# Feed-forward pass: gathers moved between POOL's power and its additions, a broadcast tensor operand on VectorE, and a later turn of h in the gated layers

## The reference

```
edge_index = jnp.stack([src, dst])
x = _layernorm(x + _L0_gnn_ref(x, edge_index, edge_attr_32, ...), axis=-1)
x = _layernorm(x + _L1_gnn_ref(x, edge_index, ...), axis=-1)
x = _layernorm(x + _L2_gnn_ref(x, ..., edge_index), axis=-1)
x = _layernorm(x + _L3_gnn_ref(x, edge_index, L3_gnn_weight), axis=-1)

# _L0_gnn_ref, after attention; `out` is the attended sum of each node
x = layer_norm(x + out, ln1_g, ln1_b)
h = x @ f1W + f1b
h = jax.nn.gelu(layer_norm(h, lnf_g, lnf_b), approximate=False)
h = h @ f2W + f2b
x = layer_norm(x + h, ln2_g, ln2_b)

# _L2_gnn_ref
h = x @ lin_w.T + lin_b
for i in range(3):
    m = h @ weight[i]
    agg = jax.ops.segment_sum(m[src], dst, num_segments=n_nodes)
    h = gru_cell(agg, h, w_ih, w_hh, b_ih, b_hh)   # (1 - z) * n + z * h
```

## Time and profile before

| | us |
|---|---|
| median of 3 runs | 6031.04 |
| the 3 runs | 6031.04, 6014.32, 6034.06 |
| profiled execution, its own time | 6028.9 |
| span of its instructions | 6027.0 |
| mean granted TensorE clock (share of 2.4 GHz) | 0.867 |

### The profile page before, as it was taken

How to read it: one execution, slowest core, us unless ns; L and a number is a source line. 1 busy time by engine, 2 the same in 40 slices (tenths; PEclk the granted TensorE clock), 3 DMA queues, 4 the chain that set the end, 5 groups by cost and what they waited for, 6 DMA issues and landing times. The chain is left out here.

```text
span 6027.0 us, 75672 instructions
## 1 busy us (share of the span) xinstructions
PE 4279.1 (71%) x16190; PEld 2524.1 (42%) x16190; DVE 4070.7 (68%) x13522; ACT 2924.8 (49%) x6388; POOL 3629.7 (60%) x3234
## 2 busy tenths in 40 slices
PE   6577759999997556546665679967996669836643
PEld 3244434444443333334443445534443334336643
DVE  6576659999997444457775676557665889836633
ACT  0466637777775010146665345534443446536643
POOL 4676558888885888735555660056104757855355
PEclk8788869999998777778887899988998899977877
DMA  6233323333332444456665675457545667757621
GB/s 214 66 85 80 73 70 99 99 99 99 99 99 78 62 62 63 54 141 196 193 190 162 185 211 146 131 160 214 164 141 147 176 159 211 197 162 227 183 78 54
DMA packets 767598, 802.43 MB, mean 133 GB/s; under 512 B 139632, under 2 KB 527800, under 8 KB 767018
## 3 DMA queue, kind: packets, MB, share of 16 engines
q1 hardware_dynamic: 405354, 393.44, 23.5%
q0 software_dynamic: 117504, 209.42, 15.0%
q10 hardware_dynamic: 244288, 194.72, 9.7%
HBM read 445.32 MB, written 351.92 MB: 132 GB/s over the span
## 5 line engine op out<-in xcount | busy, mean ns | idle before, releaser
L462 PE MATMUL gate_bank<-gate_ht,gate_whh 128*128 128x512 f32 x1764 | 874.6, 618 | 32.5 <-DVE gate_n L532 22.2
L925 POOL DMA_INDIRECT xh<-mean_xh,mean_pos_all x392 | 378.0, 964 | 349.0 <-DVE mean_xh L1027 158.9
L462 PEld LDWEIGHTS gate_bank<-gate_ht,gate_whh 128*128 128x128 f32 x1764 | 341.3, 202 | 413.0 <-issue 381.6
L2053 PE MATMUL back_ps_sums<-back_same,back_rows 128*128 128x512 f32 x400 | 289.5, 890 | 285.7 <-DMA back_rows<-x_a,back_idx 285.7
L151 POOL DMA_INDIRECT ffn_rows<-att_sums,ffn_idx x392 | 409.0, 1043 | 114.8 <-issue 106.3
L289 POOL DMA_INDIRECT gate_rows<-h_a,by_pos x200 | 195.8, 979 | 433.3 <-POOLq L117 327.3
L1494 PE MATMUL ffn_ps_f<-ffn_hg,ffn_f 128*128 128x512 f32 x784 | 407.1, 616 | 46.4 <-ACT ffn_hg L1671 46.4
L458 PE MATMUL gate_bank<-by_rank,gate_win 128*128 128x512 f32 x882 | 435.1, 593 | 0.0
L1487 PE MATMUL ffn_ps_u<-ffn_xs_t,ffn_up_w 128*128 128x512 f32 x784 | 387.2, 596 | 1.1 <-issue 1.1
L583 ACT ACTIVATE gate_z<-gate_bank,gate_b_rz 128x512 f32<-128x512 f32 x294 | 201.5, 686 | 351.0 <-PE gate_bank L462 221.0
L2034 POOL DMA_INDIRECT back<-back_out,back_dest x200 | 324.3, 1621 | 68.0 <-issue 60.1
(11 more groups left out here) (270 smaller groups left out, 11984.1 us busy)
## 6 DMA issues: line engine op xcount, KB each, us to landing
mean_x<-x_a SPq DMA_DIRECT2D x196, 256.0 KB
back<-blank ACTq DMA_DIRECT2D x99, 264.0 KB, 4.6
mean_rows<-back SPq DMA_DIRECT2D x98, 264.0 KB
hp<-mean_xh SPq DMA_DIRECT2D x98, 264.0 KB
gate_x<-xh SPq DMA_DIRECT2D x98, 264.0 KB
gate_hot<-hot_rows SPq DMA_DIRECT2D x100, 256.0 KB
ffn_x<-in_x_in SPq DMA_DIRECT2D x98, 256.0 KB
ffn_xr<-in_x_in SPq DMA_DIRECT2D x98, 256.0 KB
```

The source lines that it names most:

```text
L462: last = nc.tensor.matmul(bank_[:, :], whh[:, c * D:(c + 1) * D], ht[:, t.slot4, :], start=not inputs, stop=True)
L925: nc.gpsimd.indirect_dma_start(out=g["xh"][:, :], out_offset=bass.IndirectOffsetOnAxis(ap=pos_all[:, t.n, j:j + 1], axis=0), in_=xh[:, t.n ...
L2053: last = nc.tensor.matmul(ps_sums[t.slot][:, :], rows[:, t.slot4, j, :], same[:, t.slot, j, :], start=j == 0, stop=j == J - 1)
```

## The change

In `ffn_pass`, POOL's gathers of tile s go to the front of its step; since the steps follow each other, they now stand between the power of the step before and the two additions. DVE makes `xh` with `scalar_tensor_tensor`, whose second operand is the column of `inv` broadcast over 128 columns, where it was `tensor_scalar` with that column as a scalar.

In `gated_layer`, PE turns `hn` of item_at(3) instead of item_at(2), and all that follows comes a step later: the copies and stores, in gate2 the addition, statistics, power, shift, application, reload and scatter. `hn` gets four slots instead of two. The steps at the end grow by one.

```
@@ gated_layer
-        d, hn = (f.sb(s, [P, 2, SUPER]) for s in ("d", "hn"))
+        d, hn = f.sb("d", [P, 2, SUPER]), f.sb("hn", [P, 4, SUPER])
...
-        stored, ht_stored = f.sems("stored"), f.sems("ht_stored")
+        stored, ht_stored = f.sems("stored"), f.sems("ht_stored", 4)
...
-                if final and (t := item_at(5)) and t.has:
+                if final and (t := item_at(6)) and t.has:
                     wait(sp, stored[t.m % 2], 16 * (t.m // 2 + 1))
                     wait_alone(sp, back_scattered[t.m % 4], 64 * (t.m // 4))
                     sp.dma_start(back_x[:, t.m % 4, :, :], part_tile(x_out, HT + t.m, 0, D)
...
-                if final and (t := item_at(5)):
+                if final and (t := item_at(6)):
                     ln.rstd(nc, pool, t, y_done)
                 if e := edges_at(0):
                     sums.gather(pool, e)
-                if final and (t := item_at(6)) and t.has:
+                if final and (t := item_at(7)) and t.has:
...
-                if t := item_at(2):
+                if t := item_at(3):
                     wait(pe, h_done, t.n + 1)
                     wait(pe, out_done, t.n)
                     for j in range(J):
                         last = nc.tensor.transpose(ps_out[:, j * D:(j + 1) * D],
-                                                   hn[:, t.slot, j * P:(j + 1) * P], g["ident"][:, :])
+                                                   hn[:, t.slot4, j * P:(j + 1) * P], g["ident"][:, :])
...
-                    wait(dve, h_turned, t.n - 1)
+                    wait(dve, h_turned, t.n - 3)
                     if not final:
-                        wait(dve, ht_stored[t.slot], 16 * t.u)
+                        wait(dve, ht_stored[t.slot4], 16 * t.u4)
...
-                if final and (t := item_at(5)):
+                if final and (t := item_at(6)):
                     ln.shifts(nc, dve, t, y_done)
-                if final and (t := item_at(2)):
+                if final and (t := item_at(3)):
                     wait(dve, h_turned, t.n + 1)
...
-                if not final and (t := item_at(2)):
+                if not final and (t := item_at(3)):
                     wait(act, h_done, t.n + 1)
-                    act.dma_start(ht_out[t.tile], hn[:, t.slot, :]).then_inc(ht_stored[t.slot], 16)
+                    act.dma_start(ht_out[t.tile], hn[:, t.slot4, :]).then_inc(ht_stored[t.slot4], 16)
@@ ffn_pass
             def step(tile_at):
+                if t := tile_at(0):
+                    gather_step(nc, pool, t, idx, rows, g["att_sums"], idx_loaded, a_done, gathered)
                 if t := tile_at(2):
                     wait(pool, gathered[t.slot4], 64 * (t.u4 + 1))
...
-                if t := tile_at(0):
-                    gather_step(nc, pool, t, idx, rows, g["att_sums"], idx_loaded, a_done, gathered)
...
-                        last = nc.vector.tensor_scalar(xh[:, t.slot4, j, :], a[:, t.slot4, j, :],
-                                                       mv[:, root_slot(t, LN1), LN1, j, 0:1], inverse(t, LN1)[:, j:j + 1],
-                                                       ALU.subtract, ALU.mult)
+                        last = nc.vector.scalar_tensor_tensor(
+                            xh[:, t.slot4, j, :], a[:, t.slot4, j, :], mv[:, root_slot(t, LN1), LN1, j, 0:1],
+                            inverse(t, LN1)[:, j:j + 1].broadcast_to([P, D]), ALU.subtract, ALU.mult)
```

More of the change, by code:

```diff
@@ L420, in step @@
                                  ).then_inc(back_loaded[t.m % 4], 16)
-            over_items(5 if final else 0, step)
+            over_items(6 if final else 0, step)
             if initial:
@@ L444, in step @@
                             in_=back_x[:, t.m % 4, j, :], in_offset=None).then_inc(back_scattered[t.m % 4], 16)
-            over_items(6, step)
+            over_items(7 if final else 0, step)
             if final:
@@ L498, in step @@
                     sums.sum(pe, e)
-            over_items(2, step)
+            over_items(3, step)
         @block.vector
@@ L521, in step @@
                     wait(dve, d2_done, t.n + 1)
-                    wait(dve, h_turned, t.n - 1)
+                    wait(dve, h_turned, t.n - 3)
                     if not final:
-                        wait(dve, ht_stored[t.slot], 16 * t.u)
-                    nc.vector.tensor_tensor(hn[:, t.slot, :], d[:, t.slot, :], n3[:, t.slot, :],
+                        wait(dve, ht_stored[t.slot4], 16 * t.u4)
+                    nc.vector.tensor_tensor(hn[:, t.slot4, :], d[:, t.slot, :], n3[:, t.slot, :],
                                             ALU.add).then_inc(h_done, 1)
@@ L556, in step @@
                     nc.vector.tensor_copy(g["node_at"][:, HT:NT, :], g["tails"][:, HT:NT, :, 0]).then_inc(ids_made, 1)
-            over_items(5 if final else 2, step)
+            over_items(6 if final else 2, step)
         @block.scalar
@@ L572, in step @@
                                          ).then_inc(id_done, 1)
-                if final and (t := item_at(6)):
+                if final and (t := item_at(7)):
                     wait(act, stored[t.slot], 16 * t.u)
@@ L602, in step @@
                     nc.scalar.activation(ht[:, t.slot4, :], ps_in[:, :], ACT.Copy).then_inc(ht_made, 1)
-                if final and (t := item_at(6)):
+                if final and (t := item_at(7)):
                     wait(act, y_done, t.n + 1)
                     act.dma_start(part_tile(x_out, t.tile, 0, D), y[:, t.slot, :, :]).then_inc(stored[t.slot], 16)
-            over_items(6 if final else 2, step)
+            over_items(7 if final else 3, step)
             for b in range(2):
                 act.wait_ge(stored[b], 16 * (NT // 2))
-                if not final:
-                    act.wait_ge(ht_stored[b], 16 * (NT // 2))
+            if not final:
+                for b in range(4):
+                    act.wait_ge(ht_stored[b], 16 * ((NT - b + 3) // 4))
 class Turn:
```

## The result

| | before | after |
|---|---|---|
| median of 5 runs, us | 6031.04 | 6071.81 |
| lowest to highest, us | 6004.67 to 6037.95 | 6054.24 to 6077.97 |
| profiled execution, its own time, us | 6028.9 | 6054.2 |
| span of its instructions, us | 6027.0 | 6052.4 |
| mean granted TensorE clock | 0.867 | 0.862 |

The changed kernel is slower: ratio 1.0076, 95% interval 1.0059 to 1.0093. The forecast was 6090, with 6030 to 6150 around it; the time lies inside, 18 us under the forecast and 3 us under its narrower span of 6075 to 6110. The profiled execution of after is the fastest of its five, so the two traces lie only 25 us apart where the medians lie 41 apart.

The account below looks back on a forecast made before the run. The prediction took POOL's own sum to set ffn's 10.74 us step. From the profiled 6028.9 us it added 53 for ffn_pass and 8 for gate2, giving 6090; range 6030 to 6150, narrower span 6075 to 6110 with chance 0.52.

Parts of the forecast that it names:

- What bounds ffn: In ffn_pass: POOL's own sum of power, additions and gathers sets the 10.74 us step; POOL never waits for another engine.
- The slack that the prediction gave DVE: In ffn: removing the 2.0 us stall raises DVE's slack from 0.9 to 2.9 us a step and buys no time.
- The wait for row numbers: In ffn: the first gather starts 0.67 us later a step, as its index load is issued behind xr, which waits for xb.
- the bound of +1.33: In ffn: upper bound on the first gather's wait, 1.33 us a step, from an index load taking 3.93 us.
- The company of the gathers: In ffn: DVE operations beside gathers delay them 0.36 us a step instead of 0.43, so -0.07; bounds -0.43 and +1.8.
- +53: ffn_pass: net loss of +0.60 us a step over 88 steps, steps 10 to 97.
- (c): Rival in ffn: the load waits but gathers run undisturbed, +21 and 8, giving 6058 us; chance 0.10.
- gate0 and gate1, 0: Gated layers gate0 and gate1: turning h later changes nothing, 0 us.
- the halves bound by transfers: First halves of gate0 and gate1: they move the same bytes at 213 and 214 GB/s, so no change in time.
- gate2, +8: Layer gate2: about -4 us in the first half and +12 in the second, net +8; bounds -4 and +20.
- forecast +12: gate2's second half: the first scatter comes two steps of about 6.2 us later, +12, reaching the end as POOL is full.
- The lost lead of `x`: gate2: the load of x loses a step of lead before ACT reads it; ACT's idling hides some 2 us of waiting.

Follow-up runs that it names:

- e2: The kernel before with only xh's operand changed to the tensor form; ratio to before 0.9973, ffn_pass 1107.5 us.
- e10: The changed kernel without its new POOL order: gathers behind the additions again, xh's tensor operand and the later turn of h kept; ratio to before 0.9960.
- e1: The kernel before with only POOL's order in ffn_pass changed; ratio to before 1.0079, ffn_pass 1171.4 us.
- e3: The kernel before with only the gated layers changed (h turned a step later); ratio to before 0.9981.
- e4: The changed kernel with SP issuing the row numbers of the next tile a step earlier; ratio to before 0.9969, ffn_pass 1113.9 us.
- e9: The changed kernel with SP issuing x before the row numbers, so these come later; ratio to before 1.0196, ffn_pass 1253.6 us.

## Why the prediction was right, and where not

**What bounds ffn.** Right: POOL's own sum. The 2.0 us of DVE's stall bought nothing by going away, as forecast: in the step shown DVE idles 3.00 us in its place. The slack that the prediction gave DVE, 2.9 us, was not there in the 15 steps in which `var` stood still; these cost POOL 0.12 us each.

**The wait for row numbers, +0.67 a step.** Right in a plain step: 0.86 less 0.17 is 0.69 in the step shown, and 0.67 in the median of the steps. Too small in the mean, +0.88 (0.82 before the first gather and 0.06 before the second), because of a tail that the prediction had only as a bound: in 12 of 87 steps the gap is 1.50 us or more, which is the bound of +1.33 over 0.17, and up to 2.46. In 13 steps the load of the row numbers takes 2.9 to 4.1 us where 2.46 is the median. That also answers the 2.0 us that the prediction cites from the Trainium skill ("DMA: Bandwidth & Descriptors", Anatomy of one DMA): the section gives it for a DMA that POOL issues, this load is SP's, and none of the 87 took under 2.30 us. One of these late loads:

```profile
1232.76 2.93 POOL L1462 TENSOR_TENSOR ffn_inv<-ffn_var,ffn_power 128x16 f32<-128x16 f32 x1
1238.15 1.02 POOL L151 DMA_INDIRECT ffn_rows<-att_sums,ffn_idx  x1 [2.46 <-DMA ffn_idx<-ptr_dst]
```

**The company of the gathers, -0.07 a step.** Mis-sized: -0.28 (4 x 1.055 to 4 x 0.984). The step that failed was "now the first gather falls among the `xh`, the second at the end of the `z`: I take about the same". The first gather starts at 1316.47, late in the `xh` (1315.65 to 1316.80), since it is 0.86 us late, and neither gather is stretched much. The reading of the earlier trace rows behind it, 0.32 us because of `z`, fell in e2. What stretches the second gather is not settled; its place against `z` is the same within 0.1 us in before and in e2, and e10 has both lengths.

The two misses have opposite signs: -0.28 + 0.88, and +0.04 of the additions (1.261 and 1.254 to 1.281 and 1.271 us), give 0.64, with overlaps 0.59; forecast 0.60. So +53 came out to the microsecond, partly by luck. Of the rivals, (c), the load waits and the gathers run nearly undisturbed, describes the trace better than the forecast did.

The rule cited there, from the Trainium skill ("SBUF — State Buffer", SBUF: two separate sides), that a DVE operation with two SBUF inputs competes only with a GpSimd operation that reads SBUF, is borne out by e2 against the additions: `xh` with two tensors waits for them, 2.96 us. Against gathers the traces do not decide it: with `z` beside it, the second gather takes 1.01 us in e2, 1.27 in before and 1.01 or 1.27 in e10. The same page (Who interferes with whom) lets a tensor_reduce run free on trn2. The trace of after agrees: beside the additions, `prod`'s sum takes 0.67 us. So do `u` and `y2t`, which read PSUM, with the 1.12 and 0.74 us that they always take. POOL and DVE of after:

```profile
1310.23 1.29 POOL L1445 TENSOR_TENSOR ffn_a<-ffn_rows,ffn_x 128x512 f32<-128x512 f32 x1
```

```profile
1310.28 1.12 DVE L1640 SCALAR_TENSOR_TENSOR ffn_u<-ffn_ps_y,ffn_mv,ffn_g 128x128 f32<-128x128 f32 x4
1311.32 0.67 DVE L1647 TENSOR_REDUCE ffn_mv<-ffn_prod 128x4 f32<-128x512 f32 x1
1311.91 0.74 DVE L1581 SCALAR_TENSOR_TENSOR ffn_y2t<-ffn_ps_f,ffn_f2b,ffn_x1t 128x512 f32<-128x512 f32 x1
```

**gate0 and gate1, 0.** Not borne out, but not clearly wrong: -4 and -11 in the two profiles, on the 5588 chip -1 to -2 in gate0 and 0 to -4 in gate1 between e1, e2 and e3, e4, with one stretch of unchanged code moving by 9. The step in doubt is "the halves bound by transfers [hold] the same bytes": the bytes are the same, but the time is transfers plus pauses, which the later turn may shrink. e3's whole gain of 10 us is 4 to 6 of gate2 and a rest that no run gives to one layer.

**gate2, +8.** Wrong, -5.5. (The 70.7 us that the prediction gives as PE's wait are, in the earlier trace rows, those of its weight load.) Three terms. The first scatter does come later against the last gather: the last gather of edges ends at 4949.63, the first scatter starts at 5010.83, 61.2 us, where it was 52.0 before, +9.2 (forecast +12):

```profile
4948.69 0.94 POOL L289 DMA_INDIRECT gate_rows<-h_b,by_pos  x1 [0.30 <-issue]
...
5010.83 1.04 POOL L441 DMA_INDIRECT x_a<-gate_back_x,node_at  x1 [7.25 <-issue]
...
5317.82 0.96 POOL L441 DMA_INDIRECT x_a<-gate_back_x,node_at  x1 [0.30 <-issue]
```

The first half gave back 11.7 us (365.9 to 354.2 from the first hn to the fiftieth), not 4: short waits of DVE of some 0.1 us a step are not in the sum of waits, and the longer steps of over 7.7 us, 13 of 49 before, are down to one. Before, and then after, two `hn` in a row lie 7.42 and 7.32 us apart:

```profile
4806.68 0.69 DVE L525 TENSOR_TENSOR gate_hn<-gate_d,gate_n 128x512 f32<-128x512 f32 x1
...
4814.10 0.69 DVE L525 TENSOR_TENSOR gate_hn<-gate_d,gate_n 128x512 f32<-128x512 f32 x1
```

```profile
4829.25 0.69 DVE L525 TENSOR_TENSOR gate_hn<-gate_d,gate_n 128x512 f32<-128x512 f32 x1
...
4836.57 0.69 DVE L525 TENSOR_TENSOR gate_hn<-gate_d,gate_n 128x512 f32<-128x512 f32 x1
```

And the scatters, first to last, took 308.0 us instead of 312.4: "as POOL is full from there on" was true of before only on the average, since its first tiles came 6.3 to 7.0 us apart. Counted from the fiftieth `hn` the first scatter comes 10.7 us later, and -11.7, +10.7 and -4.4 add up to the -5.5. The lost lead of `x` was forecast as up to 2 us of hidden waiting; it is 3.7, and hidden.

**The sum.** 6028.9 + 53 - 20 gives 6062 against the profile's own 6054, the rest being the untouched passes; in the medians the change is +41, of which e1 (1.0079, 48 us at 6031) and e3 (0.9981, -11) make 37.

## What to carry to other kernels

Before an operation is moved ahead, look at what feeds its inputs in the issuing queue, not only at what it follows: here 2 KB of row numbers stood behind a load that waits for the very engine that needs them, and issuing them a step earlier turned a loss of 0.8% into a gain of 0.3%, of which about 0.2% are the gated layers' (e3). The new order by itself wins nothing even then: e4's pass, 1113.9 us, is no shorter than those of the old order with the new operand (1107.5 in e2, 1113.2 in e10), and only with `var` as a sum does it come to 1105. An engine's stall that costs nothing may move when the order changes, and fall on a small operation on the path (0.17 us became 2.10). A load with no margin pays for its tail as well as for its median.

## What the hardware showed beyond that

The late loads of row numbers go with loads of program code. Of the 87 loads from step 11 on in after, 18 had a packet of the instruction queue in flight in the 2.5 us behind their issue. They landed after 3.26 us in the mean, and 12 of the 13 that took over 2.9 us are among them; the other 69 took 2.47. e1 repeats it: 3.18 with, 2.44 without, and all 13 late ones with. It is not the only thing that slows them: in e9, where the load stands behind `x`, 29 of the 33 over 2.9 us had no such packet. The store that ACT issues was in flight in most of either kind (57 of 69 quiet loads, at 2.47). In the long step shown above, the queues between 1233.2 and 1237.4 us (packets, MB, share of 16 engines), of which the last is the code:

```profile
q1 hardware_dynamic: 428, 0.52, 46.9%
q10 hardware_dynamic: 130, 0.23, 15.6%
q8 instruction: 1, 0.02, 1.8%
```

That the packet causes the delay is an association over two traces, no run removed it.

POOL's additions, with two tensors in SBUF, stop on DVE both tensor_scalar (one tensor; `xh` in before, `var` in e4) and scalar_tensor_tensor with two tensors in SBUF (`xh` in e2) until both additions are over. They do not stop `y2t` (0.74 us) and `u` (1.12 for four), which read PSUM, nor a tensor_reduce (0.67).

A loop of two engines that hand each other a value each step can run in two ways with one program. After does: 15 steps in which DVE never waits for the power and `var` stands still beside the additions, then, behind a step of 12.69 us in which POOL pauses 1.96 us before its second gather, steps in which DVE waits for the power. e1 does the same: 8 stalled steps, the last of 11.98 us with 1.48 us of wait for row numbers. e4 has neither kind of delay (its gap is 0.19 us in every step) and stays in the first way for 87 steps. It looks as if a delay of POOL ends it, by letting DVE get ahead; that is argued from three traces, and no run puts a delay in on purpose.
